# One table for the order of a batch's work on TensorE and VectorE, and router moments kept in their own partitions

## What is computed

```python
x = L0_attn_x                                  # (8, 1024, 256)
xn = _layernorm(x)
x = x + attention(xn) + ffn(xn)
# attention: a second layer norm with ln_w, ln_b; q, k, v projections, 16 heads of 16, rotary
#   embedding on q and k; softmax(q k^T / 4) v; output projection Wo, and its own input added
# ffn: affinity = softmax(xn @ gate_w) over 8 experts; each expert takes its 256 best tokens of a
#   batch (top_k), computes (silu(x Wg) * (x Wu)) Wd, scales by the gate and scatter-adds the rows
```

## Time and profile before

| | us |
|---|---|
| median of 3 runs | 1709.43 |
| the profiled execution | 1710.81 |
| its span, first to last instruction | 1708.6 |
| TensorE busy | 1664.3 (97%) |
| ScalarE busy | 1192.4 (70%) |
| VectorE busy | 1074.9 (63%) |
| GpSimd busy | 510.2 (30%) |
| mean granted TensorE clock | 0.994 of full |

### The profile page before, as it was taken

One profiled execution on the slowest core, in us unless ns is written; L12 is line 12 of the kernel. 1 busy time (PEld: TensorE's weight loads), 2 busy tenths in 40 slices (PEclk: granted clock), 3 DMA queues, 4 the chain that ended last, 5 costly groups with the idle time before them and its releaser, 6 DMA issues.

```text
span 1708.6 us, 29033 instructions
## 1 busy us (share of the span) xinstructions
PE 1664.3 (97%) x11128; PEld 946.7 (55%) x11128; DVE 1074.9 (63%) x2350; ACT 1192.4 (70%) x1416; POOL 510.2 (30%) x480
## 2 busy tenths in 40 slices
PE   6799999999999999999999999989999999999997
PEld 5234344334434433433434433368888888888886
DVE  9874586487577477568568558866545555454543
ACT  5798988998998899899899899943333333333322
POOL 3121121101201111112112100046565565656563
PEclk9899999999999999999999999999999999999999
DMA  5645745755674585476465475255443443534332
GB/s 189 156 109 118 150 108 117 166 119 106 169 151 107 126 173 127 113 154 138 120 142 141 107 137 129 42 161 119 77 96 65 91 99 59 102 59 96 65 56 31
DMA packets 113987, 196.08 MB, mean 115 GB/s; under 512 B 20896, under 2 KB 59680, under 8 KB 113696
## 3 DMA queue, kind: packets, MB, share of 16 engines
q1 hardware_dynamic: 83696, 143.01, 36.6%
q0 software_dynamic: 29040, 49.83, 14.9%
q10 hardware_dynamic: 1088, 1.05, 0.2%
HBM read 117.27 MB, written 76.55 MB: 113 GB/s over the span
## 4 chain that ended last, share of the span: by engine, by line
PE 92%; DVE 5%; DMA 1%; POOL 1%; issue 1%; ACT 0%; POOLq 0%; SPq 0%; DVEq 0%; ACTq 0%
PE o_ps L1030 28%; PE score L1112 20%; PE score L1016 20%; PE side L899 5%; PE score L1124 5%; PE o_ps L1124 3%; PE side L909 3%; PE side L1124 2%; PE side L940 2%; PE score L1099 2%; PE side L883 1%; PE side L890 0%; DMA probs<-in_x 0%; PE side L921 0%; DMA qk<-xn_rows,rot 0%
## 5 line engine op out<-in xcount | busy, mean ns | idle before, releaser
L801 ACT ACTIVATE probs<-score 128x1024 f32<-128x1024 f32 x1024 | 968.5, 1067 | 102.8 <-PE score L1016 100.6
L1030 PE MATMUL o_ps<-probs,v_ones 128*32 128x512 f32 x4096 | 522.9, 603 | 2.2 <-DVE o_sb L1508 2.2
L1016 PE MATMUL score<-q_stack,k_stack 50*128 50x512 f32 x2048 | 395.2, 457 | 5.1 <-issue 4.5
L1016 PEld LDWEIGHTS score<-q_stack,k_stack 50*128 50x128 f32 x2048 | 163.7, 185 | 352.6 <-ACT probs L801 309.1
L785 ACT ACTIVATE probs<-score 128x512 f32<-128x512 f32 x128 | 76.6, 599 | 329.0 <-PE score L1112 322.5
L704 POOL DMA_INDIRECT out<-probs,rot x128 | 203.3, 1589 | 210.6 <-DVE probs L1473 181.3
L1458 DVE TENSOR_TENSOR probs<-score,probs 128x512 f32<-128x512 f32 x128 | 88.4, 691 | 205.6 <-PE score L1112 140.8
L1030 PEld LDWEIGHTS o_ps<-probs,v_ones 128*32 128x32 f32 x4096 | 92.2, 108 | 200.9 <-issue 139.1
L682 POOL TENSOR_TENSOR square<-qk 128x512 bf16<-128x512 f32 x56 | 77.3, 1408 | 387.4 <-DVE qk L1311 387.4
L1112 PE MATMUL score<-k_stack,q_stack 128*128 128x512 f32 x640 | 158.6, 390 | 0.0
L693 POOL DMA_INDIRECT qk<-xn_rows,rot x128 | 131.6, 1028 | 38.3 <-issue 29.5
(11 more groups left out here) (285 smaller groups left out, 2549.9 us busy)
## 6 DMA issues: line engine op xcount, KB each, us to landing
q_parts<-parts SPq DMA_DIRECT2D x16, 1024.0 KB, 4.3
k_parts<-parts SPq DMA_DIRECT2D x16, 1024.0 KB, 7.4
q_stack<-q_parts SPq DMA_DIRECT2D x62, 256.0 KB, 7.3
k_stack<-k_parts SPq DMA_DIRECT2D x62, 256.0 KB, 8.7
q_stack<-q_parts SPq DMA_DIRECT2D x66, 128.0 KB, 7.7
k_stack<-k_parts SPq DMA_DIRECT2D x66, 128.0 KB, 8.3
o_sums<-o_sb SPq DMA_DIRECT2D x256, 32.0 KB
num<-o_sums SPq DMA_DIRECT2D x32, 256.0 KB
```

Source lines behind the costliest of these rows:

```text
L801: act.activation(probs[probs_of(b, s)][:, 2 * i:2 * i + 2, :], score[ring_of(b, p)][:, :, :], ACT.Exp, scale=SCALE).then_inc(exp_done, 1)
L1016: last = pe.matmul(score[ring_of(b, p)][:, w, :], k_stack[par][rows, i, kt * P:(kt + 1) * P], q_stack[par][rows, i, qh * HALF:(qh + 1) * H ...
L1030: last = pe.matmul(o_ps[j * KEYS_W:(j + 1) * KEYS_W, :], v_ones[par][:, kt, j, :], probs[probs_of(b, s)][:, j, :], start=kt == 0, stop=kt ...
```

## The change

A table, `NEXT_ORDER`, now orders a batch: letters S and P, TensorE's jobs, and VectorE's tasks. Both engines walk it: TensorE takes the letters and the jobs, VectorE the jobs' drains, the tasks, and `copy_o` at every eighth P. Batch 0 gets the same table without the entries of a batch before it (`FIRST_ORDER`, with `sum_gate` put ahead of the first logits); batch 7 gets a table made by a rule (`LAST_ORDER`). The lag of P stays at two steps.

```diff
-    NEXT_JOBS = {4: ("z", 0, 0), 5: ("z", 0, 1), 6: ("logits", 0),
...
+    NEXT_ORDER = ("S", ("norm1", 0), "SSPP", "SSS", ("norm2", 0), "P", "SP", "SSP", "S", ("stats2", 0), "SP", "SP",
+                  "S", ("norm3", 0), "SS", ("z", 0, 0), "P", "SS", ("invert", 1), "P", "S", ("norm1", 1), "SP",
+                  ("z", 0, 1), "SSSPP", "SSS", ("logits", 0), "P", "SSS", ("qk", 0, 0), "P", "SSS", ("quarters", 0),
...
+    FIRST_ORDER = [entry for entry in NEXT_ORDER if entry not in ONLY_PREV]
+    FIRST_ORDER.insert(FIRST_ORDER.index(("logits", 0)), ("sum_gate",))
+    LAST_AROUND = {10: ("wo", 0), 16: ("wo", 1), 24: ("wo", 2), 31: ("wo", 3)}
+    LAST_ORDER = []
+    for c in range(STEPS // 2):
+        LAST_ORDER += ["SS", ("last", c)]
+        if c in LAST_AROUND:
+            LAST_ORDER += ["PPSS", LAST_AROUND[c]]
+        else:
+            LAST_ORDER += ["PSSP"] + {0: [("top",)], 28: [("lists",)]}.get(c, [])
```

TensorE's walk, and VectorE's:

```diff
+            for entry in order_of(b):
+                if is_job(entry):
+                    pe.wait_ge(side_free, jobs.before(entry))
+                    run_job(jobs, entry, nxt, prev, side[:, :])
+                elif isinstance(entry, str):
+                    for letter in entry:
+                        if letter == "S":
...
+                            score_pair(b, p)
+                            p += 1
+                        else:
+                            weigh_past(b, s, prev)
+                            s += 1
...
+                if is_job(entry):
+                    take(jobs, entry, nxt, prev, side[:, :])
+                elif not isinstance(entry, str):
+                    alongside(b, nxt, prev, jobs, *entry)
+                else:
+                    for letter in entry:
...
+                            if s >= 0 and s % KT == KT - 1:
+                                copy_o(b, s // KT)
+                            elif s == -1 and prev is not None:
+                                copy_o(prev, 2 * NG - 1)
+                            s += 1
```

The router: the logits matmul reads its tokens in strides, so that the block transpose puts each token into its own partition, and the 16 copies go:

```diff
+            return turned.rearrange("p (s q i) -> p q s i", s=HT, i=KEYS_W)[:, t]
...
-                    last = pe.matmul(bank[t * KEYS_W:(t + 1) * KEYS_W, 0:P], gate_sb[:, c, :],
-                                     xnT[:, c, t * P:(t + 1) * P], start=c == 0, stop=c == DC - 1)
+                    last = pe.matmul(bank[t * KEYS_W:(t + 1) * KEYS_W, 0:P].rearrange("e (s i) -> e s i", s=HT),
+                                     gate_sb[:, c, :], same_lanes(xnT[:, c, :], t), start=c == 0, stop=c == DC - 1)
...
-            for s in range(HT):
-                for t in range(HT):
-                    last = dve.tensor_copy(moments_of[t * KEYS_W:(t + 1) * KEYS_W, :, s],
-                                           moments[s * KEYS_W:(s + 1) * KEYS_W, :, t])
-            last.then_inc(moments_turned, 1)
+            dve.tensor_copy(moments_of[:, 0, :], mv2[:, :, 0])
+            dve.reciprocal(moments_of[:, 1, :], rstd2[:, :]).then_inc(moments_kept, 1)
```

More of the change, by code:

```diff
@@ new lines, in program, with is_job @@
+    for c in range(STEPS // 2):
[4 more added lines that the diff above has]
+            LAST_ORDER += ["PSSP"] + {0: [("top",)], 28: [("lists",)]}.get(c, [])
+    def is_job(entry):
+        return not isinstance(entry, str) and entry[0] in JOB_KINDS
+    NEXT_JOBS, SECOND_JOBS, LAST_JOBS = ([entry for entry in order if is_job(entry)]
+                                         for order in (NEXT_ORDER, FIRST_ORDER, LAST_ORDER))
@@ L316, in program, with __init__ @@
     class Jobs:
[L319 to L321 removed]
+        def __init__(self, base, order):
+            self.base = base
             self.offset = {job: i for i, job in enumerate(order)}
@@ L803, in attend @@
                 for th in range(2):
-                    if nxt is not None and s == 2 * ROUTER_CYCLE[th] + 1:
+                    if nxt is not None and s == ROUTER_STEP[th]:
                         router(nxt, th)
@@ L1043, in attend @@
             jobs = jobs_of(b)
[L1044 to L1067, removed]
-                    job = jobs.by_cycle[c]
-                    pe.wait_ge(side_free, jobs.before(job))
-                    run_job(jobs, job, nxt, prev, side[:, :])
+            p, s = 0, -LAG
+            for entry in order_of(b):
[5 more added lines that the diff above has]
+                        if letter == "S":
+                            if p % GROUP_PAIRS == 0:
+                                open_group(b, p // GROUP_PAIRS, wide)
+                            score_pair(b, p)
[3 more added lines that the diff above has]
+                            s += 1
         pe.wait_ge(const_in, CONSTS * DMA)
@@ L1562, in take_top, with alongside, alongside_last @@
                 dve_t.mark(dve.match_replace(top_scores, top_gate[:, eight], top_scores, -1.0))
+        def alongside(b, nxt, prev, jobs, what, *args):
+            if what == "norm1":
+                norm1(nxt, *args)
+            elif what == "norm2":
+                norm2(nxt, *args)
+            elif what == "stats2":
+                stats2(nxt, *args)
+            elif what == "norm3":
+                norm3(nxt, *args)
+            elif what == "affinities":
+                affinities(nxt, *args)
+            elif what == "products":
+                products(jobs, *args)
+            elif what == "rotary":
+                rotary(args[1])
+            elif what == "split":
+                split(nxt, *args)
+            elif what == "value_peak":
+                value_peak(jobs, *args)
+            elif what == "quarters":
+                quarter_split(prev, *args)
+            elif what == "invert":
+                invert((b, prev)[args[0]], args[0])
+            elif what == "sum_gate":
+                sum_gate()
+            else:
+                alongside_last(b, prev, *args)
+        def alongside_last(b, prev, c):
+            if c == 7:
+                invert(prev, 1)
+            if c in LAST_SPLIT_CYCLE:
+                quarter_split(prev, LAST_SPLIT_CYCLE.index(c))
+            for op in range(TOPS_DONE[c], TOPS_DONE[c + 1]):
+                take_top(op)
+            if c == LISTS_CYCLE:
+                order_lists()
+            if c == 30:
+                invert(b, 0)
+            if c in LOW_CYCLE:
+                if c == LOW_CYCLE[0]:
+                    dve.wait_ge(parts_out, NB * 2 * PARTS_DMA)
+                first_cast(LOW_CYCLE.index(c))
+                low_weights(0, LOW_CYCLE.index(c))
         def attend(b, nxt, prev):
@@ L1715, in _ @@
         first("v", 3)
-        value_peak(first_jobs)
+        value_peak(first_jobs, 0)
+        value_peak(first_jobs, 1)
         first("square", 1)
```

190 lines of the change are left out of this document (83 added, 107 removed), and 3 rows, old and new, of the table NEXT_JOBS.

## The result

The changed kernel took 1712.6 us (median of 20 runs, 1708.6 to 1716.9) against 1708.8 for the kernel before (20 runs, 1708.0 to 1711.5). The ratio of the two is 1.0020 (95% interval 1.0013 to 1.0026): a little slower, by 3.8 us. The forecast was 1712.1, which is 2.7 us above the 1709.43 that was then known of the kernel before. The spread of the runs grew from 3.6 to 8.3 us, which no step of the forecast had foreseen.

A forecast was written before the change was run, and what follows sets the result against it. TensorE was taken to bound middle batches after a ScalarE-paced start, ScalarE batch 7, with VectorE late in batch 0; -10.9 + 11.0 + 2.6 = +2.7 us gave 1713.5 profiled, 1712.1 median, range 1705 to 1720.

The forecast's parts named there:

- signs of failure: Product 8 of batch 0 before 79 us, a middle batch above 135 or below 133, or one waiting for `o_sb`.
- same: Whole kernel: a median from 1706.0 to 1712.8 us, within 0.2% or 3.4 us, counts as no change; chance 0.42.
- +11.0 forecast: Batch 0: product 8 +6.4, first `qk` +2.6, five S in a row +3.7, fewer runs -1.7; range +5 to +14 us.
- -10.9 forecast: Batches 1 to 6: 1.9 us gained in each, less 0.7 at the change from batch 0; range -3 to -14.
- (a): TensorE, middle batches: runs of P fall from 48 to 38 at 0.15 us each, 0.36 given back; net 1.1 saved a batch.
- (b): TensorE, middle batches: S ahead of P at the start means fewer waits for ScalarE; 0.8 us saved a batch.
- Later S runs: Middle batches, after the 15th S: tighter S runs wait for barely finished exponentials; allowance of 0.8 us a batch.
- +2.6 forecast: Batch 7: copies behind list operations delay product 8 by 1.0 and product 24 by 1.6 us; range 0 to +4.
- 0.2 in hand: Batch 7, product 8: two exponentials (1.84 us) against P and their start (1.60) leave 0.2 us of cover.
- C: Rival, middle batches: the copy behind `norm1`, waiting for `xin`, holds product 8; 3.5 us a batch, 1733 in all; chance 0.13.
- D: Rival, TensorE: joined runs bring nothing, or strides eat the gain; 7 x 1.2 = 8.5 us goes, 1720; chance 0.12.
- B: Rival, batch 0: the `xin` load lands sooner, 73.1 instead of 79.7; 5.2 us less, total 1706.8; chance 0.20.

The follow-up runs named there:

- e2: Changed kernel with VectorE's order in batch 0 altered: gate's sum earlier, second half's `norm1` behind the copy and second drain; ratio 1.0008 to the kernel before.
- e4: Changed kernel with each `SSSPP` of the table cut into `SSPSP` in batches 1 to 6, 42 more runs of P; ratio 1.0096 to the kernel before.
- e3: Changed kernel with batch 7's copy of `o_ps` put ahead of its cycle's list operations; ratio 1.0015 to the kernel before.
- e1: Changed kernel with `invert` of the batch before moved behind the copy and the second transposes' drain; ratio 1.0016 to the kernel before.
- f1: Kernel before with the router part alone: moments kept in their own partitions, 16 small copies a half gone, strided logits matmul; ratio 0.9987 to the kernel before.
- f4: f3 with the next-but-one batch's first `xin` load issued some 10 us later, after v job 2 is drained; ratio 0.9966 to the kernel before.
- f3: Changed kernel with its own batch 0 table, `invert` behind the second transposes, and batch 7's copy ahead of list operations; ratio 0.9957 to the kernel before.

## Why the prediction was right, and where it was not

The total was right by luck in good part. The three terms of the sum (batches 1 to 6, batch 0, batch 7) missed by +4.5, -1.7 and -1.5 us, and these errors cancel to 1.3. Two of the forecast's own signs of failure came: batch 3 took 137.1 us, above 135, and five middle batches waited for `o_sb`. And the measured difference to the kernel before, 3.8 us, lies outside the 3.4 that the forecast called "same"; the 1712.6 lies inside its band only because the kernel before measured 0.7 lower this time.

**Batch 0 (+11.0 forecast, +9.3 measured).** The chain was as forecast: `norm1` waiting for `xin`, the copy behind it. `xin` landed 9.8 us after its issue, not 11.2, so product 8 came at 80.6, not 82.3. But its price was wrong. TensorE waited 1.83 us at product 8, where 5 to 8 were forecast and 1.71 had been recorded before (not the one wait for `o_sb` there, as the forecast reads it: three more, of 0.15 to 0.23 us, are recorded in batches 4 and 7); and e2, which takes this wait and that at the first `qk` away, gives back 3.5 us, where the two terms were 6.4 + 2.6 = 9.0. Most of the delay had already met TensorE at the first transposes (3.8 us from piece to piece), a wait that I had not named: the new order reaches them 5 products into the batch, where it was 10. The first `qk` waited 0.6, not 2.6. The runs of five S cost 1.4 to 1.5 each, 4.4 in all (3.7 forecast). The fewer runs gave 14 x 0.34 less what the logits' P gives back, some 4.4, not 1.7. And behind the waits at the transposes and at product 8 the clock fell, which I had left out (below): the pieces there took 1.4 us longer each time.

**Batches 1 to 6 (-10.9 forecast, -6.4 measured).** Two sizes were off, in opposite directions. (a) The term for runs: 10 x 0.15 - 0.36 = 1.1 a batch was forecast; by e4 it is 10 x 0.30, and by the rows of S and P 10 x 0.34, so 3.0 to 3.4. (b) The term for waits, a saving of 0.8, was wrong in sign. I summed, for each piece of TensorE, its time above the shortest such piece with the same neighbours: 14.3 us in the six batches before, 29.2 after. In a clean batch it is 2.4 before and 3.8 after. The start of the batch went as forecast: the 15th S comes 11.77 us after the first (11.75 forecast), with 0.5 of waits where there were 1.1. What failed is the allowance of 0.8 for the "Later S runs": behind the 15th S the waits grew from 1.3 to 3.3, because runs of three S overtake the three buffers (0.3 to 0.6 us at the 27th and at the 41st S in nearly every batch). Over the eight batches the profile records 22 waits of an S for `probs`, 7.4 us together, where that of before has one of 0.3. The other 6 us are the waits at product 8 behind `invert`, with the slow clock behind the longest of them. Per clean batch the new order gains 135.8 - 133.6 = 2.2, near the 1.9 forecast, though by other sizes: 3.6 of less work in TensorE's pieces (135.8 - 2.4 against 133.6 - 3.8) less 1.4 of more waiting.

**Batch 7 (+2.6 forecast, +1.1 measured).** TensorE stood still for 1.3 and 1.65 us, near the 1.0 and 1.6 that were worked out as net costs. But ScalarE caught up part of each: e3 shows 0.6 and 1.0 of them in the batch's length, 1.6 in all, so "0.2 in hand" was too little. And without them the new order is 0.5 better than before, which I had not counted.

**The rivals.** C had the right place, the copy ahead of product 8 in the middle batches, and the wrong load: `den` by way of `invert` (e1). Its price was 0.4 to 3.6 us in five of six batches, where C said 3.5 in each. D is refuted by e4 for the runs, and by f1 for the strides (0.3 us in six batches, where D had 1.2 in each). The rule of the Trainium skill that stood for D ("TensorE: Matmul & The Clock Gate", section "Step-by-step: what each phase is for": the next weights load beside the running matmul) does not make this switch free: the runs show 0.30 to 0.34 us for each pair of runs. B fails: the load in batch 0 came 1.4 us sooner, not 6.6. The moments are worth nothing in the middle batches (f1), as forecast. So in the middle batches a gain of runs that was forecast three times too small stands against waits that the forecast did not have: those of the runs of three S, and those behind `invert`.

**Open.** The spread of the runs (8.3 us against 3.6) is not settled. The kernel before spread by 6.2 us itself over its 29 runs beside e1 to e4, and by 4.5 over the 22 beside f1 to f4. The profiles of kernels with the same code in these batches give 808.4, 808.3, 805.1 and 807.7 for the six, with a cost at product 8 of anything from 0 to 3.6 us in a batch. That accounts for some 3 us of spread and the rest after the last S for another 2.8. In f3 the five runs spread by 1.9 us, in f4 six by 3.7, too few to say more.

## What to carry to other kernels

When two engines walk one table, each task in it inherits every wait of the tasks ahead of it: before moving one, list which loads those tasks wait for, and put what the bounding engine needs (here a 0.7 us copy) ahead of all of them. Price a switch between two kinds of work on both sides, by runs of one, two and three of each in the trace. Do not add up waits that lie one behind another: a delay that meets the engine early is not met again later, and an engine with work in hand catches up part of it. And a table derived by leaving entries out (batch 0 without `wo`) is a new order, with its own clumps and its own late engine.

## What the runs showed of the hardware

Some waits of TensorE cost more than their length. After the 1.8 us wait in batch 3 the granted clock was 0.50 for 3.1 us, and two P took 3.4 us instead of 1.86; after the 3.6 us wait in batch 0 it was 0.58. Windows of the changed kernel, the wait ahead of product 8 of batch 3 and the time behind it:

```profile
482.50:484.40 1.90, 0.07 (x3) 0.01 (x1) 1.86 (x9) 1.90 (x3) 0.46 (x2) 0.95 0.97 114
484.40:487.50 3.10, 3.10 (x16) 0.58 (x16) 3.03 (x4) 0.43 (x1) 0.81 (x1) 0.50 1.10 159
```

That is 1.2 GHz where it had run at 2.4. In batch 3 a wait of 2.0 us from piece to piece became 3.6 us. Behind the recorded waits of 1.1 and 1.46 us in batch 7, the products kept their full-speed durations (1.06 and 1.07 us); so did the product behind the 1.71 us of the earlier trace rows. The length of the wait does not decide alone. In e1 the same wait of 1.46 us stands ahead of the same product 24 of batch 7. The two windows of each pair start just ahead of the wait and 3.8 us later; first e1, then the changed kernel:

```profile
1050.20:1051.90 1.70, 0.25 (x2) 0.00 (x0) 1.67 (x5) 1.70 (x3) 0.00 (x0) 1.00 0.64 217
1054.00:1057.00 3.00, 3.00 (x18) 0.75 (x20) 2.90 (x8) 2.13 (x3) 0.00 (x0) 0.63 0.58 117
```

```profile
1052.90:1054.60 1.70, 0.28 (x2) 0.00 (x0) 1.67 (x5) 1.70 (x3) 0.00 (x0) 1.00 0.62 213
1056.70:1059.70 3.00, 3.00 (x28) 0.91 (x24) 2.92 (x7) 3.00 (x4) 0.00 (x0) 1.00 0.51 108
```

The clock is 0.63 in e1 and 1.00 in the changed kernel, and the 1.3 us that batch 7 took longer in e1 arise there, between the 55th and the 61st S. The clock also fell behind the 1.32 us wait in batch 3 of e1 (0.67, then 0.64). So one and the same order cost 1.3 us more in one execution than in another, and what decides it is open here.

The landing time of one and the same 1 MB store, the second `k_parts` of a batch, was 6.5 to 10.3 us. With the 512 KB load issued 1.6 us ahead it was 8.1 to 10.3 (batches 1 to 5 of the changed kernel, e1 to e3 and f3); with that load 2.4 us behind, 7.3 to 8.2 (the kernel before); with it 9 us behind, 6.5 in four batches of f4, 7.2 and 8.2 in the others. The load itself landed after 5.3 to 6.9 us ahead of the store of batch 2, and after 11.9 in f4, where the loads of the stacks are issued beside it. The Trainium skill, "DMA: Bandwidth & Descriptors", section "Issuing engines are not separate DMA queues", says that transfers of all issuers interleave on the same 16 engines; these landing times agree.
